# Edge stages of a graph layer: loads and stores on separate queues, four gather buffers, loops of four chunks, and a last layernorm summed in PSUM

## The reference

```python
xn = layernorm(x)
# two graph attention convolutions, 4 heads of 64 features each, self loops added
def gat_conv(x, src, dst, W, a_src, a_dst, b):
    h = (x @ W).reshape(-1, H, C)
    e = leaky_relu(alpha_s[src] + alpha_d[dst], 0.2)      # alpha = (h * a).sum(-1)
    ex = exp(e - segment_max(e, dst)[dst])
    alpha = ex / (segment_sum(ex, dst)[dst] + 1e-16)
    return segment_sum(h[src] * alpha[:, :, None], dst).reshape(-1, H * C) + b
gnn = gat_conv(relu(gat_conv(xn, ...W1...)), ...W2...)
# linear attention, 8 heads of 64: k and v normalised per head
mix = (q @ (k.T @ v) / n) @ Wout.T + bout
x = x + gnn + mix
# mixture of experts, the best 2 of 16, then a layernorm with gamma and beta
x = x + layernorm(y + moe(y)) * gamma + beta              # y = layernorm(x)
```

## Time and profile before

| | |
|---|---|
| time, median of 3 runs | 3418.54 us (3417.31 to 3422.86) |
| profiled execution | 3409.54 us, its span 3407.9 us |
| mean granted TensorE clock | 0.815 |
| busy: PE, DVE, ACT, POOL | 2115.9, 1824.2, 1317.3, 1848.1 us |
| share of the span | 62%, 54%, 39%, 54% |
| first edge stage | gathers from 200.5 to 1430.6 us, 784 of them |
| second edge stage | gathers from 1488.2 to 2762.5 us, 784 of them |
| `finish` | about 3326 to 3400 us |

### The profile page before, as it was taken

One profiled execution on the slowest core, in us unless ns is written; L12 is line 12 of the kernel. 1 busy time (PEld: TensorE's weight loads), 2 busy tenths in 40 slices (PEclk: granted clock), 3 DMA queues, 4 the chain that ended last, 5 costly groups with the idle time before them and its releaser, 6 DMA issues. The chain is left out here.

```text
span 3407.9 us, 55844 instructions
## 1 busy us (share of the span) xinstructions
PE 2115.9 (62%) x11635; PEld 1691.8 (50%) x11636; DVE 1824.2 (54%) x5645; ACT 1317.3 (39%) x2599; POOL 1848.1 (54%) x1918
## 2 busy tenths in 40 slices
PE   0737777666676676736555555555455646999980
PEld 0425555445455554524444444444344435999970
DVE  3655555455555555555455445444555456555547
ACT  0524444444444444412333333333333323444434
POOL 0246665556666665536555555555555621666653
PEclk9968878788888887867777777777777777999995
DMA  2623333333333333344333333333333325556544
GB/s 51 214 70 98 99 98 93 92 93 98 97 96 99 97 97 94 83 128 107 102 101 105 104 97 101 101 101 103 98 103 103 105 63 153 104 104 105 103 83 154
DMA packets 245728, 348.90 MB, mean 102 GB/s; under 512 B 87442, under 2 KB 184105, under 8 KB 245513
## 3 DMA queue, kind: packets, MB, share of 16 engines
q0 software_dynamic: 101728, 251.76, 29.8%
q1 hardware_dynamic: 124249, 72.10, 8.0%
q10 hardware_dynamic: 19552, 23.24, 2.1%
HBM read 292.90 MB, written 54.42 MB: 102 GB/s over the span
## 5 line engine op out<-in xcount | busy, mean ns | idle before, releaser
L921 POOL DMA_INDIRECT gathered<-table,idx x1568 | 1496.3, 954 | 1020.7 <-issue 447.6
L1201 PE MATMUL psA_e<-gathered,hotf 128*128 128x260 f32 x3136 | 913.9, 455 | 7.6 <-issue 7.0
L1201 PEld LDWEIGHTS psA_e<-gathered,hotf 128*128 128x128 f32 x3136 | 725.8, 236 | 151.4 <-issue 10.0
L1193 PE MATMUL psT<-identb,hot 128*128 128x128 bf16 x1568 | 164.7, 268 | 774.9 <-DVE hot L958 767.8
L1193 PEld LDWEIGHTS psT<-identb,hot 128*128 128x128 bf16 x1568 | 122.0, 120 | 790.2 <-issue 701.3
L975 DVE TENSOR_TENSOR gathered<-gathered,psW_e 128x2048 f32<-128x2048 f32 x98 | 224.2, 2288 | 261.4 <-issue 211.2
L1093 ACT ACTIVATE hotf<-hot 128x1024 f32<-128x1024 bf16 x196 | 207.0, 1056 | 385.9 <-DVE hot L958 374.2
L1097 ACT ACTIVATE hotT<-psT 128x1024 bf16<-128x1024 bf16 x196 | 200.0, 1021 | 387.6 <-DMA x_in<-in_x 374.9
L975 DVE TENSOR_TENSOR gathered<-gathered,psDW_e 128x2048 f32<-128x2048 f32 x98 | 224.2, 2288 | 204.3 <-issue 110.8
L958 DVE TENSOR_SCALAR hot<-iota,code_r 128x128 bf16<-128x128 bf16 x1568 | 279.3, 275 | 70.0 <-issue 68.2
L1612 POOL DMA_INDIRECT moe_d<-xscaled,xtarget x113 | 179.3, 1587 | 121.0 <-DMA moe_d<-xscaled,xtarget 44.4
(11 more groups left out here) (306 smaller groups left out, 2961.1 us busy)
## 6 DMA issues: line engine op xcount, KB each, us to landing
gathered<-table,idx POOLq DMA_INDIRECT x1568
w<-in_L_ffn_w ACTq DMA_DIRECT2D x8, 2048.0 KB
xb<-in_L_ffn_b SPq DMA_DIRECT2D x113, 128.0 KB
w<-xnT_d SPq DMA_DIRECT2D x98, 128.0 KB
xf_d<-w SPq DMA_DIRECT2D x50, 128.0 KB
moe_d<-w SPq DMA_DIRECT2D x50, 128.0 KB
table<-acc POOLq DMA_DIRECT2D x49, 130.0 KB, 2.6
table<-acc SPq DMA_DIRECT2D x49, 130.0 KB
```

The source lines that it names most:

```text
L921: pool.indirect_dma_start(out=G[:, q, k, :], out_offset=None, in_=table, in_offset=bass.IndirectOffsetOnAxis(ap=idx[:, q, k:k + 1], axis=0 ...
L1193: ins = pe.transpose(psT[:, k, :], hot[:, q, k, :], identb[:])
L1201: ins = pe.matmul(psA[:, par, 0:GW], hotf[:, q, k, :], G[:, q, k, :], start=(k == 0), stop=(k == KT - 1))
```

## The change

- SLOTS goes from 3 to 4: four buffers for the gathered rows, the indices and the float one-hots. A new TURN = 2 is the number of buffers of what belongs to a tile (x, xnT, vs) and of `hot`, `hotT`, `dwin` and `half`, which go by the parity of the chunk. The signals that started at SLOTS for the tile's buffers start at TURN.
- The loop's body is four chunks.
- SP issues loads only. The stores of the table, and of xf_d and moe_d, go to ACT's queue, at offset 9. The stores of the pad rows move to the start of the second stage.
- SP's load of xnT has offset 1 in the first stage (0 before) and 6 in the second (3 before).
- DVE's `weigh` is cut into `edge_logits`, which comes first in the step, and `edge_scale`; `exps` comes ahead of `floats` and `turned` on ACT, `targets` first on PE.
- What follows the sums of a tile comes a step later on all engines. In the first stage `values` has offset 3 and `keys` 4 on PE (1 and 2 before).
- In `finish` DVE computes (x - mean) * gamma in one instruction, ACT scales the identity by 1/std, and PE sums in PSUM the identity times `acc` and that diagonal times the centred rows; ACT copies the result. The shift, the product with gamma and the sum on DVE go.

```diff
@@ -32,7 +32,8 @@
-SLOTS = 3
+SLOTS = 4
+TURN = 2
@@ -183,8 +184,8 @@
-            vs = [w1[:, 11 + b, 0] for b in range(SLOTS)]
-            xnT = [w1[:, 4 + b, 0, 0:C] for b in range(SLOTS)]
+            vs = [w1[:, 11 + b, 0] for b in range(TURN)]
+            xnT = [w1[:, 4 + b, 0, 0:C] for b in range(TURN)]
@@ -758,12 +759,12 @@
-        dwin = sb("dwin", [P, SLOTS, 6 * H], BF16)
-        half = sb("half", [P, SLOTS, 6 * H], BF16)
+        dwin = sb("dwin", [P, 2, 6 * H], BF16)
+        half = sb("half", [P, 2, 6 * H], BF16)
...
-        hot = sb("hot", [P, SLOTS, KT, P], BF16)
+        hot = sb("hot", [P, 2, KT, P], BF16)
...
-        hotT = sb("hotT", [P, SLOTS, KT, P], BF16)
+        hotT = sb("hotT", [P, 2, KT, P], BF16)
@@ -831,17 +832,17 @@
                 def told(step):
-                    return lambda c, k, u: step(r * NC + c, c, k % SLOTS, k % 2, r * len(range(k % SLOTS, NC, SLOTS)) + u * 2 + k // SLOTS)
+                    return lambda c, k, u: step(r * NC + c, c, k, k % 2, r * len(range(k, NC, SLOTS)) + u)
...
                     def even(c, k, u):
...
-                            step(r * NT + (u * SLOTS + b), u * SLOTS + b, b, r * len(range(b, NT, SLOTS)) + u)
+                            step(r * NT + (u * TURN + b), u * TURN + b, b, r * len(range(b, NT, TURN)) + u)
...
-                skewed(eng, NC, 2 * SLOTS, 2, 2, [(o, tile_of(step) if by_tile else told(step)) for o, step, *by_tile in stages])
+                skewed(eng, NC, SLOTS, 2, 2, [(o, tile_of(step) if by_tile else told(step)) for o, step, *by_tile in stages])
@@ -879,16 +880,14 @@
-                def store(t, i, b, use):
-                    d = dest_of(sp, i)
-                    sp.wait_ge(s["out"], t * 2 + 6)
-                    sp.dma_start(table_out[ds(i * P, P), :], acc[:, ds(d, 1), :].rearrange("p o f -> p (o f)")).then_inc(s["stored"], 16)
-                rounds = chunks(sp, both_new(sp), nothing, (0, load), (0, load_x, True), (8, store, True))
+                rounds = chunks(sp, new_pass(sp), nothing, (0, load), (1, load_x, True))
...
+                for rows in (xf_d, moe_d):
+                    sp.dma_start(rows[NT * P:(NT + 1) * P, 0:C], mixM[:, 0, :]).then_inc(s["constants"], 16)
@@ -897,14 +896,7 @@
-                def store(t, i, b, use):
-                    sp.wait_ge(s["xf"], t + 2)
-                    sp.dma_start(xf_d[ds(i * P, P), 0:C], xf).then_inc(s["stored"], 16)
-                    sp.dma_start(moe_d[ds(i * P, P), :], xf).then_inc(s["stored"], 16)
-                rounds = chunks(sp, both_new(sp), nothing, (0, load), (3, load_x, True), (8, store, True))
-                for rows in (xf_d, moe_d):
-                    sp.dma_start(rows[NT * P:(NT + 1) * P, 0:C], xf).then_inc(s["constants"], 16)
-                sp.wait_ge(s["constants"], 112)
+                rounds = chunks(sp, new_pass(sp), nothing, (0, load), (6, load_x, True))
@@ -955,12 +947,12 @@
             def one_hot(g, c, q, par, use):
...
-                    dve.tensor_scalar(hot[:, q, k, :], iota[:], code_r[:, ds(c * KT + k, 1)], None, ALU.is_equal).then_inc(s["hot"], 1)
+                    dve.tensor_scalar(hot[:, par, k, :], iota[:], code_r[:, ds(c * KT + k, 1)], None, ALU.is_equal).then_inc(s["hot"], 1)
...
-                blend(dve, chain, dwin[:, q, :], half[:, q, :], parts, tile, lower[:, ds(c, 1)], upper[:, ds(c, 1)]).then_inc(s["dwin"], 1)
...
-            def weigh(g, c, q, par, use):
+                blend(dve, chain, dwin[:, par, :], half[:, par, :], parts, tile, lower[:, ds(c, 1)], upper[:, ds(c, 1)]).then_inc(s["dwin"], 1)
...
+            def edge_logits(g, c, q, par, use):
@@ -969,6 +961,8 @@
+            def edge_scale(g, c, q, par, use):
@@ -1012,15 +1006,15 @@
-                    dve.wait_ge(s["dots"], t + SLOTS)
+                    dve.wait_ge(s["dots"], t + TURN)
...
-                rounds = chunks(dve, both_new(dve), next_pass, (0, one_hot), (4, keys, True), (1, weigh), (2, gain), (4, denominators, True), (3, sums, True))
...
-                hold(dve, s["dots"], rounds * NT + SLOTS, s["tick"])
+                rounds = chunks(dve, both_new(dve), next_pass, (1, edge_logits), (0, one_hot), (6, keys, True), (1, edge_scale), (3, gain), (5, denominators, True), (5, sums, True))
...
+                hold(dve, s["dots"], rounds * NT + TURN, s["tick"])
@@ -1050,10 +1044,10 @@
-                dve.wait_ge(s["constants"], 80)
+                dve.wait_ge(s["constants"], 112)
...
-                rounds = chunks(dve, both_new(dve), next_pass, (0, one_hot), (7, scales, True), (1, weigh), (2, gain), (4, denominators, True), (6, stats, True), (6, with_beta, True))
+                rounds = chunks(dve, both_new(dve), next_pass, (1, edge_logits), (0, one_hot), (8, scales, True), (1, edge_scale), (3, gain), (5, denominators, True), (7, stats, True), (7, with_beta, True))
@@ -1090,11 +1084,11 @@
             def floats(g, c, q, par, use):
...
-                act.activation(hotf[:, q, :, :], hot[:, q, :, :], ACT.Copy).then_inc(s["hotf"], 1)
+                act.activation(hotf[:, q, :, :], hot[:, par, :, :], ACT.Copy).then_inc(s["hotf"], 1)
...
             def turned(g, c, q, par, use):
...
-                act.activation(hotT[:, q, :, :], psT[:], ACT.Copy).then_inc(s["hotT"], 1)
+                act.activation(hotT[:, par, :, :], psT[:], ACT.Copy).then_inc(s["hotT"], 1)
@@ -1106,15 +1100,15 @@
-                act.wait_ge(s["fin_turned" if attention else "mixed"], t + (1 if attention else SLOTS))
+                act.wait_ge(s["fin_turned" if attention else "mixed"], t + (1 if attention else TURN))
...
                 def squares(t, i, b, use):
-                    act.wait_ge(s["keys_ps"], t + 1 + SLOTS)
-                    act.wait_ge(s["values_ps"], t + 1 + SLOTS)
+                    act.wait_ge(s["keys_ps"], t + 1 + TURN)
+                    act.wait_ge(s["values_ps"], t + 1 + TURN)
@@ -1138,10 +1132,15 @@
+                def store(t, i, b, use):
+                    d = dest_of(act, i)
+                    act.wait_ge(s["out"], t * 2 + 6)
+                    act.dma_start(table_out[ds(i * P, P), :], acc[:, ds(d, 1), :].rearrange("p o f -> p (o f)")).then_inc(s["stored"], 16)
...
-                chunks(act, new_dest(act), nothing, (4, roots, True), (5, divide, True), (0, floats), (0, turned), (3, squares, True), (1, exps), (6, relu, True), (7, copies, True))
+                chunks(act, new_dest(act), nothing, (9, store, True), (6, roots, True), (1, exps), (0, floats), (0, turned), (6, divide, True), (5, squares, True), (7, relu, True), (8, copies, True))
@@ -1164,10 +1163,15 @@
                 def gates(t, i, b, use):
...
+                def store(t, i, b, use):
+                    act.wait_ge(s["xf"], t + 2)
+                    act.dma_start(xf_d[ds(i * P, P), 0:C], xf).then_inc(s["stored"], 16)
+                    act.dma_start(moe_d[ds(i * P, P), :], xf).then_inc(s["stored"], 16)
...
-                chunks(act, new_dest(act), nothing, (7, root, True), (11, gates, True), (9, xf_turned, True), (5, divide, True), (0, floats), (0, turned), (1, exps), (7, normalise, True))
+                chunks(act, new_dest(act), nothing, (9, store, True), (8, root, True), (1, exps), (0, floats), (0, turned), (12, gates, True), (10, xf_turned, True), (6, divide, True), (8, normalise, True))
@@ -1183,14 +1187,14 @@
-                    ins = pe.matmul(psD[:, 2 * k:2 * k + 2, :, :].rearrange("p g c h -> p (g c h)"), hotT[:, q, k, :], dwin[:, q, :], start=True, stop=True)
+                    ins = pe.matmul(psD[:, 2 * k:2 * k + 2, :, :].rearrange("p g c h -> p (g c h)"), hotT[:, par, k, :], dwin[:, par, :], start=True, stop=True)
...
             def turn(g, c, q, par, use):
...
-                    ins = pe.transpose(psT[:, k, :], hot[:, q, k, :], identb[:])
+                    ins = pe.transpose(psT[:, k, :], hot[:, par, k, :], identb[:])
@@ -1236,11 +1240,11 @@
-                pe.sem_inc(s["dots"], SLOTS)
-                pe.sem_inc(s["values_ps"], SLOTS)
-                pe.sem_inc(s["keys_ps"], SLOTS)
+                pe.sem_inc(s["dots"], TURN)
+                pe.sem_inc(s["values_ps"], TURN)
+                pe.sem_inc(s["keys_ps"], TURN)
...
-                chunks(pe, nothing, nothing, (5, dots, True), (1, targets), (0, turn), (7, project, True), (6, fin_turn, True), (2, add), (1, values, True), (2, keys, True))
+                chunks(pe, nothing, nothing, (1, targets), (8, project, True), (0, turn), (7, fin_turn, True), (7, dots, True), (2, add), (3, values, True), (4, keys, True))
@@ -1275,11 +1279,11 @@
-                pe.sem_inc(s["mixed"], SLOTS)
+                pe.sem_inc(s["mixed"], TURN)
...
-                pe.wait_ge(s["constants"], 80)
+                pe.wait_ge(s["constants"], 112)
...
-                chunks(pe, nothing, nothing, (8, fin_turn, True), (6, mix, True), (10, gates, True), (1, targets), (0, turn), (2, add))
```

(63 more changed lines are left out.)

16 lines of the change are left out of this document (8 added, 8 removed).

## The result

The changed kernel takes 3476.86 us (median of 4 runs, 3475.69 to 3488.91); the kernel before took 3420.7 beside it (4 runs, 3417.31 to 3435.2). The ratio is 1.0164, with a 95% interval of 1.0127 to 1.0201: slower by 1.6%, 56 us, where 3456 was forecast. The profiled executions differ by more, 3474.1 - 3407.9 = 66.2 us of span, because that of before, 3409.54 us, lies 11 us under its median.

The account below looks back on a forecast made before the run. The prediction took GpSimd's gathers, 10.0 us a chunk, plus a drain gap of about 2.5 us before PE's signals get through, as the bound. Terms +115 - 15 - 60 - 16 + 14 + 0 = +38 us gave 3456 us, range 3335 to 3525.

Parts of the forecast that it names:

- The index wait: First edge stage: index loads queue behind xnT's wait for keys, 2.4 us for each of 48 tiles, +115 us.
- The -15 for the fourth buffer: First edge stage: a fourth buffer removes the gap's excess over a 2.55 us floor, -15 us.
- gaps of 2.5 and 5 in turn: First edge stage: expected profile sign, gaps alternating about 2.5 and 5, the long ones released by the index DMA.
- my upper bound: First edge stage, index wait: the 1.88 us of keys wholly behind the drain, 206 us in all.
- The drain: Edge stages: each chunk needs a gap of about 2.5 us before PE's signals get through; more buffers alone don't remove it.
- a sign against its law: Edge stages: gaps of 0.30 in number would show that the drain isn't a law.
- four buffers free GpSimd: Rival, edge stages: gaps fall to 0.30 where a buffer is free, up to 506 us less, 2910; chance 0.06.
- The second stage: Second edge stage: fourth buffer, and logits first covering DVE's loop stall, remove the excess over the drain, -60 us.
- Logits first make a chain: Rival, edge stages: targets, logits, one-hots, turn and add follow one another, 11.5 us a step, about 3550; chance 0.10.
- The ends of the stages: Both edge stages: extra steps without gathers, less one saved drain, cost +7 us per stage, +14 in all.
- Finish: Last stage: work moves from DVE to PE and ACT, 1.40 us a tile falls to 1.07, -16 us.
- Shorter loops: Rival, edge stages: 21 turns in place of 14 with uncovered 3.73 us DVE stalls, 3546 in all; chance 0.04.

Follow-up runs that it names:

- e1: Changed kernel with SP's load of xnT in the first edge stage at offset 4 in place of 1; 3358.59 us, ratio 0.9601.
- e4: Changed kernel with three buffers in place of four and the loop of six chunks again; 3353.97 us, ratio 0.9585.
- e2: e1 with DVE's one-hots ahead of the logits again in both edge stages; 3362.9 us, ratio 0.9634.
- e6: Kernel before, with only DVE's weigh cut in two and the logits put ahead of the one-hots; 3500.93 us, ratio 1.0238.
- e5: Kernel before, with only ACT's exps moved ahead of floats and turned in both edge stages; 3396.77 us, ratio 0.9945.
- e8: Kernel before, with only the edge stages' stores issued by ACT (offset 8), pad rows at the second stage's start; 3409.96 us, ratio 0.9987.
- e3: Kernel before, with only the new finish of the changed kernel; 3470.61 us, ratio 0.9921.
- e7: e1 with ACT's exps behind floats and turned again in both edge stages; 3377.09 us, ratio 0.9882.
- e10: e1 with DVE adding a chunk's sums at offset 2 in place of 3; 3003.64 us, ratio 1.03.
- e12: e1 with a loop body of eight chunks in place of four; 2882.95 us, ratio 0.9883.

## Why the prediction came out as it did

**The index wait: right in mechanism and nearly in size.** The forecast was +115 us; without the wait, in e1, the stage is 129 us shorter. The two terms of the first stage together (+115 - 15) were +100, and measured are +121. The -15 for the fourth buffer has its like in e1 against e4, 16 us, with the loop's length altered too. The chain is the one that was worked out: from index issue to gather 2.62 us (613.90 to 616.52) against 2.63, keys to index issue 0.88 (613.02 to 613.90) against 0.53. The pattern is only in part the one that I expected, gaps of 2.5 and 5 in turn. Of the pairs of chunks, 14 show it (2.48 and 5.24 in the mean). In 29 others the first gap is 0.30 and the next 6.3 to 11.3, 7.9 in the mean: the two index loads that had waited go out together, and the pair runs through without a gap. In the stretch shown the long gap holds the keys in full, 1.9 us, which was my upper bound. Per pair of chunks the gaps, as mean of the same timeline's 97, grew from 2 x 2.67 to 2 x 3.92 us, by 2.5 us. The two terms of this stage forecast 2.1 (100 / 48), so the gap that is saved and the keys in full nearly cancel. That the sum comes so near is in part luck.

**The drain: right for the chips on which it was read, wrong as a law.** In e1 the gap is 2.6 us though PE's add ended 3.5 us before the last gather, as I had read it in the earlier trace rows. But a third of the gaps in the first stage of the changed kernel, 32 of 97 counted in GpSimd's timeline, are 0.30. Three of them are the free buffers at the start; in the other 29 the add had ended in the midst of the gathers and GpSimd still went straight on. This is what the prediction named as a sign against its law. And on the third chip there is nearly no hold. There the time is what the rival "four buffers free GpSimd" describes, but three buffers reach it as well.

**The second stage: the size right by luck, the cause wrong.** -60 was forecast, -65 measured. The reasons given were the fourth buffer and DVE's stall at the loop. e4 has three buffers and keeps all of the gain but 13 us. e2 puts the one-hots ahead of the logits again and keeps it too. e6 takes the stall away from the one-hots and is slower. e5 and e8 rule out the exponentials and the stores as the whole of it. Nor does the size hold elsewhere: on the first group's chip the stage falls from 1335 us (e3) to 1228 (e1), by 107, and on the second's from 1275 (e8) to 1241 (e7), by 34. What e1, e2, e4 and e7 share, and e5, e6 and e8 lack, is finish (which in e3, alone, leaves the stage at 1335), PE's order (the targets first), hot, hotT, dwin and half by the chunk's parity, the later load of x and xnT in this stage (offset 6 for 3), and that the sums and all behind them come a step later, so that DVE no longer stops in its step for PE's add. I had costed that at nothing. I take the later sums for the likeliest cause, by e6's and e10's waits; the others in this list, finish apart, weren't run alone. Shown is only, on the chip without held signals, that it is needed beside the logits first. That it is enough by itself on a chip that holds them is open.

**Logits first make a chain.** As a rival it was given 0.10 and 11.5 us a chunk. In the changed kernel it doesn't close; in e6 and e10, where the sums come a step earlier, it does, for 2.4% of the kernel before and 4.2% of e12.

**The ends of the stages: too small.** +7 each was forecast, measured +19 and +14. I had taken a step without gathers at the 7.2 us of the earlier trace rows. In the changed kernel the step at that place takes 12.4 us:

```profile
1552.72 0.36 DVE L958 TENSOR_REDUCE both_e<-psDW_e 128x64 f32<-128x192 f32 x1 [4.66 <-PE psDW_e L1190]
...
1565.13 0.36 DVE L958 TENSOR_REDUCE both_e<-psDW_e 128x64 f32<-128x192 f32 x1 [4.27 <-PE psDW_e L1190]
```

In this step each engine waits for the next: the two waits shown are for PE. The order of logits and one-hots is not what makes the end long, though: in e2, with the one-hots first, the steps there take 7.1 us, and from the last gather to the next stage's first 76 pass all the same. By e1 and e4 the fourth buffer costs 15 us there (75.4 against 60.7), the later sums 2 (60.7 against 58.5).

**Finish: right in direction, too small.** -16 forecast, -22 measured. The mis-sized terms are PE and ACT, which were to take 1.03 us a tile each: four records on PE, which I took from the earlier trace rows as the time from the first start to the last end, take 0.87 in a dense row, and ACT's three instructions 0.83. DVE, forecast at 0.92, takes 0.84.

**Shorter loops.** DVE's stall at the turn of the loop no longer stands ahead of the one-hots in the changed kernel, and a stage with four chunks to a turn keeps pace with its gap. By the Trainium skill, page "Runtime: NRT & Kernel Launch", section "Instruction fetch mechanics", such a stall comes with each taken branch out of the loaded window; the traces agree that there is one at each turn (e6 shows it moved to the logits, 25.9 us in 600), and no run here shows that a fetch is behind it or that it cost time in the change.

The sum was +38, the measured difference of the medians 56 and of the profiled executions 66. From 38 to 66 lead the ends of the stages (+19) and the first stage (+21), less finish (-6), the second stage (-5) and the start (-1).

## What to carry to other kernels

When a load moves in an in-order queue, ask of each wait in front of it in which step of the other engine it falls; if that is the step which also frees the next buffer, everything queued behind the load pays the full latency of its own DMA. One number, the offset of a load, cost more here than all the rest of the change gained: 129 us, against the 63 that are left of them beside the measured 66. With it set to 4 the kernel is 4% faster than before on its chip. On that chip even the sign of the change is doubtful: by an estimate from these rows the changed kernel would take 3359 + 129 = 3488 us there, and the kernel before takes 3496. And where a step is reordered so that one engine's first work depends on another's last, move what waits for that other engine's next signal out of the step as well.

## What the hardware showed

The same kernel takes 2915 us on one chip, 3413 on a second and 3496 on a third, with the same instructions; beside the result, on a chip that isn't on record, it takes 3421. The traces of its variants put the difference down to how soon other engines see PE's signals while GpSimd's gathers run: 0.04 us on the first chip, up to 8.4 us in the stretch of the changed kernel shown above, where a gap of about 2.5 to 2.7 us opens behind most chunks' last gather. The kernel before has no trace on the chip of 2915 us, but the size fits: the prediction's sum for gaps of 0.30 in both stages was 506 us, and 3421 - 506 = 2915.

DVE's signals are not held, and the hold on PE's has a place. In the first stage of the changed kernel ACT stood waiting for DVE's logits 50 times while gathers ran, and saw them within 0.04 us each time. DVE stood waiting for PE's targets 55 times: of the 11 that ended during a chunk's first six gathers 9 were seen after 0.04 us, and of the 44 that ended during the last two none before 1.65 us. The profile models the ends of PE's records, so whether PE's signal is late or its last result is, these traces don't part; nor does any run show why chips differ. A gain that is read in such gaps holds for chips of that kind: e1 is 4.0% faster than the kernel before on one of them, and e12, its variant with the loop of eight, 1.2% where nearly no signal is held.
